# One-token shifts by TensorE and by an offset copy in place of SBUF transfers, with a new order of the layers' software pipeline

## What is computed

```python
def shift_tokens(t):                 # second half of the channels comes from the token before
    a, s = jnp.split(t, 2, -1)
    s = jnp.pad(s, ((0, 0), (1, 0), (0, 0)))[:, :-1]
    return jnp.concatenate([a, s], -1)
...
q, k, v = split(shift_tokens(x) @ Wqkv)
q = l2norm(q) * qs ; k = l2norm(k) * ksc
q = q * cos * scale + rotate_half(q) * sin * scale
k = k * cos / scale + rotate_half(k) * sin / scale
x = x + local_attention(q, k, v) @ Wo
xn = layernorm(shift_tokens(x)) * g + b
a, gate = split(xn @ W1 + b1)
x = x + (a * gelu(gate)) @ W2 + b2
```

## Time and profile before

| | us |
|---|---|
| median of 3 runs | 3286.9 |
| lowest, highest | 3286.65, 3301.44 |
| the profiled execution | 3307.22 |
| its span | 3305.4 |
| TensorE matmul busy | 2136.7 |
| TensorE weight loads busy | 1453.0 |
| VectorE busy | 1507.0 |
| GpSimd busy | 1395.0 |
| ScalarE busy | 1256.3 |

### The profile page before, as it was taken

The page is one execution under the profiler, slowest core; times in us unless marked ns, Lnnn a source line. Parts: engine busy times, 40 slices in busy tenths (PEclk is TensorE's granted clock), DMA queues, the critical chain, the costliest instruction groups (busy, mean ns, idle before and its releaser), DMA issues. The chain is left out here.

```text
span 3305.4 us, 84537 instructions
## 1 busy us (share of the span) xinstructions
PE 2136.7 (65%) x35763; PEld 1453.0 (44%) x35859; DVE 1507.0 (46%) x2246; ACT 1256.3 (38%) x1602; POOL 1395.0 (42%) x2271
## 2 busy tenths in 40 slices
PE   4776777486486557555864685557556855686565
PEld 1444444254354345344643464445344633454444
DVE  3333333464455444544553455436445544555442
ACT  2544555143244324333432343234223432343332
POOL 1333333464345344444443454436434544454441
PEclk7989998797798779778987898788778977898787
DMA  3999999221221113111212221131112221221111
GB/s 108 250 239 245 261 291 253 68 63 44 74 56 41 35 46 84 37 45 46 55 38 67 52 51 37 44 80 45 40 40 53 55 64 41 52 55 36 41 43 30
DMA packets 209830, 273.13 MB, mean 83 GB/s; under 512 B 81412, under 2 KB 92336, under 8 KB 208688
## 3 DMA queue, kind: packets, MB, share of 16 engines
q1 hardware_dynamic: 174640, 200.61, 22.8%
q10 hardware_dynamic: 34816, 67.12, 9.0%
HBM read 86.08 MB, written 68.29 MB: 47 GB/s over the span
## 5 line engine op out<-in xcount | busy, mean ns | idle before, releaser
L503 PE MATMUL yps<-wo,oT 128*128 128x128 f32 x1536 | 227.9, 311 | 746.6 <-DVE x L664 745.5
L245 POOL TENSOR_TENSOR roped<-turned 128x512 f32<-128x512 f32 x384 | 478.4, 1267 | 365.2 <-PE ring L442 360.3
L432 PE MATMUL ring<-wqkv,xT 128*128 128x512 f32 x1152 | 582.3, 630 | 35.2 <-DVE turned L572 27.0
L503 PEld LDWEIGHTS yps<-wo,oT 128*128 128x128 f32 x1536 | 221.6, 225 | 799.4 <-issue 797.8
L572 DVE TENSOR_TENSOR turned<-ring,ropes 128x1024 f32<-128x1024 f32 x384 | 452.2, 1220 | 259.3 <-ACT squares L310 168.8
L310 ACT ACTIVATE squares<-ring 128x1024 f32<-128x1024 f32 x192 | 196.5, 1024 | 979.6 <-DVE ss L581 668.8
L280 POOL TENSOR_TENSOR roped<-roped,rnorm 128x1024 f32<-128x1024 f32 x192 | 361.6, 1906 | 0.0
L286 POOL TENSOR_TENSOR rstd<-meanvar,eps 128x4 f32<-128x4 f32 x24 | 4.8, 201 | 806.5 <-DVE meanvar L639 806.5
L632 DVE BATCH_NORM_STATS2 stats<-xsf 128x6 f32<-128x128 f32 x96 | 20.9, 282 | 707.1 <-DMA xsf<-x 707.1
L979 POOL TENSOR_SCALAR less<-less,lowest 128x512 f32<-128x512 f32 x256 | 174.4, 692 | 389.8 <-DVE lowest L957 389.8
L957 DVE CUSTOM_DVE_ANT_0 less<-ps_b,shifted 128x512 f32<-128x512 f32 x256 | 166.7, 689 | 367.2 <-DMA shifted<-scratch_w 262.1
(11 more groups left out here) (112 smaller groups left out, 3593.7 us busy)
## 6 DMA issues: line engine op xcount, KB each, us to landing
vwin<-v SPq DMA_DIRECT2D x1536, 64.0 KB, 2.0
scratch_w<-wrows SPq DMA_DIRECT2D x128, 513.0 KB, 13.6
shifted<-scratch_w ACTq DMA_DIRECT2D x128, 512.0 KB, 13.5
wqkv<-in_l_wqkv SPq DMA_DIRECT2D x6, 1536.0 KB
xs<-x SPq DMA_DIRECT2D x24, 128.0 KB
wo<-in_l_wo SPq DMA_DIRECT2D x24, 128.0 KB
xsf<-x SPq DMA_DIRECT2D x24, 128.0 KB
xs<-x SPq DMA_DIRECT2D x24, 127.0 KB
```

The source lines that it names most:

```text
L245: nc.gpsimd.tensor_tensor(halves[2][:, :, side, :], halves[0][:, :, side, :], halves[1][:, :, 1 - side, :], ALU.add).then_inc(s[name + "_a ...
L432: last = nc.tensor.matmul(out[:, half, :], xT[:, t % 2, :], wqkv[:, layer_of(t), at + half * 512:at + (half + 1) * 512], start=True, stop= ...
L503: last = nc.tensor.matmul(out[:, 0:D], oT[:, j, :], wo[:, layer_of(t), j, :], start=j == 0, stop=j == PAIRS - 1)
```

## The change

1. The shift for the attention is made when ScalarE copies the turned tile out of PSUM: `xT` is now one buffer of 513 columns, the first 64 channels go to column t, the other 64 to column t+1; column 0 of these is zero. TensorE turns `x` itself. The copy becomes two instructions of 64 partitions.
2. The shift for the feed-forward is three matmuls per group into room 0 (`shift`, kind "XS"): the identity for the first half, and a matrix `down` that moves each row one down and the last row of a tile into the next tile. Statistics and normalisation read it from PSUM, and the room is freed by `xn_made`.
3. The six transfers per group, `xs`, `xsf` and their semaphores go. SyncE loads the first layer's weights at once, then only issues window copies and weights.
4. The rotary products wait for the projection alone; the squares on ScalarE wait for the rotary products, and now free the rooms of q and k.
5. `ROOM` is a new table, and the order within a period is new on all compute engines. `take_attended` moves to the start of the next period.

```diff
-        xs = sb("xs", [P, SEQT, D])
-        xsf = sb("xsf", [P, SEQT, D])
-        xT = sb("xT", [P, 2, P])
+        down = sb("down", [P, 2, P])
+        xT = sb("xT", [P, SEQ + 1])
...
-        FREED = {"Q": ("q_rotated",), "K": ("k_rotated",), "V": ("v_copied",), "QT": ("qT_copied",),
+        ROOM = {"S": 0, "V": 1, "QT": 0, "KT": 2, "K": 1, "PT": 2, "O": 0, "Q": 2, "OT": 1, "H0": 2, "H1": 1, "H2": 0, "XS": 0, "XT": 3, "XN": 3, "Y": 4, "F": 4}
+        FREED = {"Q": ("q_squared",), "K": ("k_squared",), "V": ("v_copied",), "QT": ("qT_copied",),
...
-            for n in PERIODS:
-                step, g = n % SEQT, n // SEQT
-                if step == 3:
-                    attention_in(g + 1)
-                    if g < 0:
-                        load_layer(0)
-                    ffn_in(g - 1)
+            load_layer(0)
+            for n in range(NT):
                 windows(n)
...
+            nc.gpsimd.tensor_copy(down[:, 0, 1:P], ident[:, 0:P - 1]).then_inc(s["ready"], 1)
+            nc.gpsimd.tensor_copy(down[:, 1, 0:1], ident[:, P - 1:P]).then_inc(s["ready"], 1)
...
-                    act.wait_ge(s[name + "_made"], t + 1)
+                    act.wait_ge(s[name + "_rotated"], t + 1)
...
-                    nc.scalar.copy(xT[:, t % 2, :], tpose[:, 0:P]).then_inc(s["xT_copied"], 1)
+                    at, half = t % SEQT * P, D // 2
+                    nc.scalar.copy(xT[0:half, at:at + P], tpose[0:half, 0:P]).then_inc(s["xT_copied"], 1)
+                    nc.scalar.copy(xT[half:D, at + 1:at + 1 + P], tpose[half:D, 0:P]).then_inc(s["xT_copied"], 1)
...
+            def shift(g):
+
+                if lives(g):
+                    pe.wait_ge(s["y_added"], SEQT * (g + 1))
+                    at, half = g % BATCH * SEQT, D // 2
+                    out = take("XS", g)[:, 0, :].rearrange("p (t d) -> p t d", d=D)
+                    nc.tensor.matmul(out[:, :, 0:half], ident[:, :], x[:, at:at + SEQT, 0:half], start=True, stop=True,
+                                     skip_group_check=True)
+                    nc.tensor.matmul(out[:, :, half:D], down[:, 0, :], x[:, at:at + SEQT, half:D], start=True, stop=False,
+                                     skip_group_check=True)
+                    nc.tensor.matmul(out[:, 1:SEQT, half:D], down[:, 1, :], x[:, at:at + SEQT - 1, half:D], start=False, stop=True,
+                                     skip_group_check=True).then_inc(s["shifted"], 1)
...
-                    dve.wait_ge(s[name + "_squared"], t + 1)
+                    dve.wait_ge(s[name + "_made"], t + 1)
...
-                    dve.wait_ge(s["xsf_in"], XSHIFT * (g + 1))
+                    dve.wait_ge(s["shifted"], g + 1)
                     for tile in range(SEQT):
-                        nc.vector.bn_stats(stats[:, tile, :], xsf[:, tile, :]).then_inc(s["stats_made"], 1)
+                        nc.vector.bn_stats(stats[:, tile, :], ring[:, room("XS"), 0, tile * D:(tile + 1) * D]).then_inc(s["stats_made"], 1)
```

More of the change, by code:

```diff
@@ L152, in load_layer @@
                     sp.dma_start(dst, src).then_inc(s["weights"], 16)
[L154 to L170, removed]
             def windows(t):
@@ L203, in _ @@
             nc.gpsimd.memset(kT[:, :, 0:W], 0.0).then_inc(s["cleared"], 1)
-            nc.gpsimd.memset(xs[0:1, :, :], 0.0).then_inc(s["cleared"], 1)
-            nc.gpsimd.memset(xsf[0:1, :, :], 0.0).then_inc(s["cleared"], 1)
+            nc.gpsimd.memset(down[:, :, :], 0.0).then_inc(s["ready"], 1)
             nc.gpsimd.memset(power[:, :], -0.5).then_inc(s["ready"], 1)
@@ L413, in take @@
                     for name in FREED[held]:
-                        pe.wait_ge(s[name], before + 1)
+                        pe.wait_ge(s[name], (before + 1) * (2 if held == "XT" else 1))
                 holder[r] = (kind, FCH * at + c if kind == "H" else at)
@@ L431, in project @@
                     for half in range(2):
-                        last = nc.tensor.matmul(out[:, half, :], xT[:, t % 2, :],
+                        last = nc.tensor.matmul(out[:, half, :], xT[:, t % SEQT * P:(t % SEQT + 1) * P],
                                                 wqkv[:, layer_of(t), at + half * 512:at + (half + 1) * 512], start=True, stop=True)
@@ L548, in _ @@
                     hidden(g - 2, 2)
-                project("V", n)
-                turn_x(n + 1)
                 turn_p(n - 2)
-                turn_qk(0, n - 1)
+                if step == 2:
+                    shift(g - 1)
+                    project_ffn(g - 2)
                 if step == 3:
                     turn_xn(g - 1)
+                project("V", n)
                 attend(n - 2)
-                turn_qk(1, n - 1)
                 project("Q", n + 1)
@@ L645, in normalise @@
                     for tile in range(SEQT):
-                        ins = nc.vector.tensor_scalar(xn[:, tile, :], xsf[:, tile, :], meanvar[:, tile, 0:1],
+                        ins = nc.vector.tensor_scalar(xn[:, tile, :], ring[:, room("XS"), 0, tile * D:(tile + 1) * D], meanvar[:, tile, 0:1],
                                                       rstd[:, tile:tile + 1], ALU.subtract, ALU.mult)
@@ L665, in add_ffn @@
                                             ALU.add).then_inc(s["x_done"], 1)
+            nc.vector.memset(xT[D // 2:D, 0:1], 0.0).then_inc(s["cleared"], 1)
             for n in PERIODS:
                 step, g = n % SEQT, n // SEQT
+                if step == 3:
+                    normalise(g - 1)
+                if step == 1:
+                    gate(g - 2, 2)
+                if step == 3:
+                    add_ffn(g - 2)
+                take_attended(n - 3)
                 rotate(0, n)
                 take_max(n - 2)
[L671 to L672 removed]
                 take_scores(n - 2)
                 rotate(1, n)
[L675 to L676 removed]
+                add_y(n - 3)
+                sum_squares(0, n)
                 if step == 0:
                     gate(g - 2, 0)
[L679 removed]
+                sum_squares(1, n)
                 if step == 0:
                     gate(g - 2, 1)
[L682 removed]
+                if step == 2:
+                    statistics(g - 1)
                 sum_probs(n - 2)
                 invert(n - 2)
[L685 to L689 removed]
             dve.wait_ge(s["x_done"], GROUPS)
```

66 lines of the change are left out of this document (28 added, 38 removed).

## The result

| | us |
|---|---|
| median of 4 runs (before, on the same chip: 3286.97) | 2450.94 |
| lowest, highest | 2441.96, 2460.15 |
| ratio to before | 0.7449 [0.7414, 0.7483] |
| the profiled execution, its span | 2449.03, 2447.2 |
| TensorE matmul busy, weight loads busy | 2091.9, 1422.6 |

The mean granted clock of TensorE is 0.961, where it was 0.843. Two kernels of the experiments have one execution each that lies far from its others (2814.8 and 5012.2 us), and their medians are taken without it.

What follows compares the result with a forecast made beforehand. The stall for the `xsf` transfers bounded the kernel, TensorE outside it. Work 69.9, gaps 3.6, stops 4.1 and clock 1.7 make 79.3 us per group; 715 us off 3307.2 gives 2592, scaled to 2580 us, range 2495 to 2740.

Steps and rivals of the forecast that it cites:

- The main term: VectorE's statistics waiting for the `xsf` transfers, 707.1 us in 24 groups, 29.5 per group, would go with the transfers.
- so the new order gives what the shift and its own gaps take: Forecast 79.3 us per group equals 79.0, the old group less the wait, so the change gains just the waits, 715 us.
- TensorE's work: Per group 69.9 us: four periods of 14.85, hidden products 5.6, last product 3.0, turn of `xn` 0.7, shift 1.2.
- low clock: TensorE's stops lower its clock; a fifth of 17 us at the low level costs 1.7 us per group.
- stops: TensorE's "issue" stops in the scores and in `attend` stay, 4.1 us per group.
- gaps: TensorE's waits in the new order, 3.6 us per group: 1.8 around turns and `attend`, 0.6 shift, 1.2 first hidden product.
- rival 2: Stops in `attend` and the scores grow as these blocks come closer: 286 us more, 2870 us; chance 0.06.
- The shift's room: Held until `xn_made`, about 4.5 us, beside 4.7 us of TensorE's last product and V before `attend` takes it.
- Other engines: VectorE's 13.5 us, its 12.5 us chain from `attend` and GpSimd's 14.4 us were to fit in the period of 15.3.
- Hand-overs through the rooms: Rival: hand-overs through the three rooms bound the period, 10 us more per group, 2810 us; chance 0.12.
- The last rival: TensorE has room, so GpSimd bounds at some 66 us per group, 2280 us; chance 0.03.
- The clock did not stay low: Rival: a TensorE that hardly rests is held at the low clock; at half of the work 3420 us; chance 0.03.

Runs made afterwards that it cites:

- The old orders without transfers: Changed kernel with the rooms, order within a period and squares' place of before, shift in the single bank behind `attend`: 2607.3 us, 80.8 per group.
- the old orders with one piece moved: Old orders without transfers, with the output product directly ahead of `attend` and its addition ahead of `take_attended`: 2494.1 us, stops in `attend` 67.6 to 24.0 us.
- the direct test: Changed kernel with V projected ahead of the turn of the probabilities, so that a short turn stands directly ahead of `attend`: 2618.6 us.
- one experiment: Changed kernel with the first hidden product behind the turn of q instead of ahead of it: 2436.0 us.
- another: Changed kernel with the shift's result in the single bank of the turned x instead of room 0: 2404.8 us.
- one added line: Kernel before with the feed-forward shift's transfers issued in step 2 ahead of the window copies: 2771.6 us.

## Why the prediction was wrong

**The main term was right.** The stall was one stall, counted once, and it went with the transfers. The old orders without transfers measured 80.8 us per group; by the forecast's subtraction (108.5 - 29.5) that kernel is 79.0 + 1.2 for the shift = 80.2, within 1%.

**The step that failed** is "so the new order gives what the shift and its own gaps take". The 79.0 held a wait that the sum had nowhere: the output product's for the feed-forward addition, 4.2 us per group in the old orders without transfers. The new order takes it away, and with it much of the low clock behind it and over half of the stops, and is worth 6.7 us per group where the forecast had it pay for the shift and its own gaps and no more. The sum of terms came out at the same 79.3 because its other terms were too large, which is luck. It is 5.2 too high, and 5.2 x 23 = 119 us. Term by term, over the 23 groups of the changed kernel:

| per group, us | forecast | measured | from |
|---|---|---|---|
| TensorE's work | 69.9 | 67.8 | 4 x 14.54 + 5.21 + 2.68 + 0.44 + 1.26, the starts above |
| low clock | 1.7 | 0.3 | what is left: 1705.1 less all waits, over 23, is 68.1; less 67.8 |
| stops | 4.1 | 1.9 | 44.7/23 |
| gaps | 3.6 | 4.1 | 93.6/23, all waits that are not "issue" |
| sum | 79.3 | 74.1 | |

- *Stops, 2.2 us too much.* I wrote that they stay (and left out 13.5 us of them at the turns of q and k, 8 times in the kernel before). Those in `attend` go by what stands directly ahead of it, as the old orders with one piece moved show, and the change put a long projection there. That this is what the projection does in the changed kernel itself is inferred, since the direct test mixed two things; and why the stops in the scores fell too, from 24.9 to 13.8 us, is open. I had listed their growth as rival 2, with "they come closer" as the reason, and saw only the direction in which they could get worse. A table of what stands ahead of the two blocks in each order would have shown the other one.
- *Work, 2.1 too much.* The plain period of 14.85 held a wait for the copy of v that I took for work:

```profile
PE ring L442 <- ACT v L345: 14.4, 68, 0.3
```

  That is a row of the kernel before, 0.2 us per period, 0.8 per group; the plain period came out at 14.54, 0.1 less still. The products counted once per group were busy sums, which overlap their neighbours and hold slow-clock matmuls: 5.6, 3.0 and 0.7 were 5.21, 2.68 and 0.44 by starts.
- *Clock, 1.4 too much.* I took the low clock of one stretch, which held a stop of 2.3 us, as the rule. Stops of 2 us and more are rare in the changed kernel, and the wait of 4.2 us is not there.
- *Gaps, 0.5 too little.* Three were close: first hidden product 28.0/23 = 1.2 (1.2), turn of the probabilities 0.9 (1.0 for the four periods), shift 0.66 (0.6). The copy ahead of `attend` cost 2.2/23 = 0.1 and not 0.8. The shift's room "just fits" by 0.2 us did not fit: `attend` waits 0.5 per group for `xn`.
- *Shift:* 1.26 us, forecast 1.2; matmuls of 256 and 192 columns do go by columns. *Other engines:* none became the bound.

**The rivals.** Hand-overs through the rooms: all gaps together are 4.1 us per group, not 10 more. The stops did not grow. The last rival, room on TensorE, was also added up wrongly: its terms, 14.4 x 4 + 1.3 + 4.1, make 63 us per group and not 66. The clock did not stay low, it rose to 0.99. The page of the Trainium skill that was weighed, Perfetto Trace Analysis, section Identifying the Most-Contended Engine, would by its rule have left room on TensorE: loads are busy 1107.41 of 1705.10 us, 65%. But matmuls are busy 92% and start one behind the other, and where waits of TensorE were taken away (17 us in one experiment, 27 in another), the groups together became 16 and 45 us shorter. The measurement decides for the matmul starts.

**What the profile was to show.** Right: no long wait of the statistics (1.3 us), none of the output product, SyncE idle between the window copies, TensorE busy above 85% at a clock above 0.9. Wrong: 79 us per group, and stops of about 100 us in all; both wrong in the same direction. The range's lower end had allowed the gaps to vanish, and nothing else to get better: the stops, the clock and the period itself needed a lower bound as well.

## What to carry to other kernels

When a stall that dwarfs all else goes, list what it hid (here a wait of 4.2 us; the sign of it was that TensorE waited longer than the engine that it waited for) and what hung on it (the low clock behind it), and give each "stays as it is" a value below as well as above. Take the cost of work from starts in a stretch without any wait, down to tenths, before multiplying it by four periods and 24 groups. And before a transfer is replaced, move its issue: one added line was worth 510 of the 836 us.

## What the runs showed of the hardware

**TensorE's program arrives in pieces.** The queue that carries the program, in the page of the changed kernel (packets, MB, share of 16 engines):

```profile
q8 instruction: 287, 4.70, 0.8%
```

4.70 MB in 287 packets are 16.4 KB each, and TensorE's 36,003 matmuls and as many loads make 251 instructions per packet, with its semaphore instructions on top. The Trainium skill, Advanced Engine Details and Errata, section ISA Cache, gives a line as 16 KB or 256 instructions; the trace agrees. A packet takes 1.05 to 1.14 us in the median of each kept trace, and in none of the twelve do two start less than 3.25 us apart. `attend` is 128 matmuls and 128 loads in 1.4 us. With a turn of 0.9 us ahead of it 256 instructions are gone well before the next packet can be there; with the eight instructions of a projection and their 1.8 us ahead it is a near thing. Two things in the records fit this. In all twelve traces every stop of over 0.4 us in the layers ends 1.1 to 1.7 us behind the end of a packet. And the stops of over 0.6 us lie at one place of the program modulo 256: matmuls and loads counted from the start, and 1.0 to 1.2 more for each change of line (one fitted number per kernel, for the semaphore instructions that the records leave out), all 16 to 71 stops of a trace are within 6.2 instructions of one value. So the stops are waits for the next 256 instructions of the program. That what stands ahead of a dense block decides how long they last was tested in the old orders alone.

**Short idle times and the clock.** In the old orders without transfers all 22 waits of 4.2 us of the output product were followed by a clock of 0.50 to 0.66 over the next 3 us, and in the one shown above the 16 records took 3.75 us, against 1.95 at full clock. Stops of 2.0 to 2.7 us in the same kernel, from 782 us on, were followed by a low clock in nine cases and by 1.00 in six, among them the 2.50 us in the row above. In the changed kernel one stop of 3.89 us was followed by 0.50. So a wait of 4 us can cost nearly 2 us more behind itself.
